# Spatial attention on TensorE: eight heads by four contiguous keys in a block, mixing on 64x32 tiles

## The reference, cut to what matters

```
q, k, v = split(layernorm(h) @ w_qkv.T + b_qkv)          # 8 heads, width 8
dots  = q . k                                            # 94 x 94 for each head
grass = (qr(q).Q . qr(k).Q) ** 2 * grassman_scale
a = concat([dots * scale, dots ** 2 * riem_scale, grass])  # 24 maps
a = batchnorm(a)                                         # constants per map
a = conv_w (8 x 24) @ a + conv_b                         # mixes the 24 maps into 8
out = softmax(a, over keys) @ v ; out @ w_proj.T + b_proj
```

## Time and profile before

| | |
|---|---|
| median of 3 runs | 1019.79 us (1017.86 to 1020.41) |
| the profiled execution | 1019.19 us, span 1017.5 us |
| TensorE matmul busy / weight load busy | 898.6 us (88%) / 577.8 us (57%) |
| VectorE busy | 763.6 us (75%) |
| GpSimd busy | 488.2 us (48%) |
| ScalarE busy | 423.6 us (42%) |
| mean granted TensorE clock | 0.944 |
| instructions | 37672 |

### The profile page before, as it was taken

One profiled execution on the slowest core, in us unless ns is written; L12 is line 12 of the kernel. 1 busy time (PEld: TensorE's weight loads), 2 busy tenths in 40 slices (PEclk: granted clock), 3 DMA queues, 4 the chain that ended last, 5 costly groups with the idle time before them and its releaser, 6 DMA issues. The chain is left out here.

```text
span 1017.5 us, 37672 instructions
## 1 busy us (share of the span) xinstructions
PE 898.6 (88%) x15018; PEld 577.8 (57%) x15018; DVE 763.6 (75%) x1287; ACT 423.6 (42%) x710; POOL 488.2 (48%) x551
## 2 busy tenths in 40 slices
PE   3677668998937999999999999999999999799995
PEld 2233245555525666666666666666666666446663
DVE  4588863887983888888788888888888888747773
ACT  2333423112713444444444444444444444257774
POOL 3355631110007666666666666666666666212220
PEclk9777877998977999999999999999999999979998
DMA  8765000324102111111111111111111111001111
GB/s 300 263 223 202 1 0 1 55 54 115 31 0 64 50 49 50 52 52 52 48 45 48 50 52 52 52 49 46 48 49 50 52 52 53 2 3 29 29 29 32
DMA packets 64446, 63.25 MB, mean 62 GB/s; under 512 B 37081, under 2 KB 55068, under 8 KB 64412
## 3 DMA queue, kind: packets, MB, share of 16 engines
q1 hardware_dynamic: 63884, 61.25, 20.4%
q10 hardware_dynamic: 528, 1.54, 0.4%
HBM read 52.93 MB, written 6.75 MB: 59 GB/s over the span
## 5 line engine op out<-in xcount | busy, mean ns | idle before, releaser
L1163 ACT ACTIVATE sq<-ps_dot 128x752 f32<-128x752 f32 x192 | 153.1, 798 | 302.6 <-PE ps_dot L1042 302.6
L1042 PE MATMUL ps_dot<-q_st,k_blk 32*64 32x94 f32 x6144 | 169.4, 247 | 3.1 <-POOL k_blk L1002 3.1
L1042 PEld LDWEIGHTS ps_dot<-q_st,k_blk 32*64 32x64 f32 x6144 | 134.4, 133 | 64.6 <-issue 50.0
L1002 POOL TENSOR_TENSOR k_blk<-k_turn,hmask 128x384 f32<-128x384 f32 x64 | 65.3, 1020 | 177.8 <-ACT k_turn L1151 177.8
L1210 DVE TENSOR_REDUCE sums<-prob 128x94 f32<-128x564 f32 x128 | 148.0, 1201 | 2.0 <-ACT prob L1156 2.0
L1006 POOL TENSOR_TENSOR k_mix<-k_cm,cols 128x768 f32<-128x768 f32 x64 | 119.8, 1872 | 0.0
L988 POOL TENSOR_TENSOR v_blk<-v_rep,vmask 128x384 f32<-128x384 f32 x128 | 106.6, 854 | 6.8 <-PE ps_m L1074 6.8
L1091 PEld LDWEIGHTS ps_a<-q_st,k_mix 64*64 64x64 f32 x3072 | 77.1, 132 | 56.4 <-issue 48.2
L1091 PE MATMUL ps_a<-q_st,k_mix 64*64 64x94 f32 x3072 | 101.0, 250 | 0.8 <-DVE prob L1198 0.8
L1156 ACT ACTIVATE prob<-prob,cols 128x564 f32<-128x564 f32 x128 | 91.1, 758 | 20.4 <-DVE prob L1198 20.4
L1181 DVE TENSOR_REDUCE row_max<-ps_a 128x94 f32<-128x564 f32 x128 | 89.3, 741 | 12.4 <-PE ps_a L1110 12.4
(11 more groups left out here) (225 smaller groups left out, 1389.7 us busy)
## 6 DMA issues: line engine op xcount, KB each, us to landing
v_rep<-v_rows SPq DMA_DIRECT2D x256, 96.0 KB
x_g<-in_x_dram SPq DMA_DIRECT2D x15, 1500.0 KB, 6.7
v_rows<-tok SPq DMA_DIRECT2D x32, 96.0 KB
q_st<-q_cm SPq DMA_DIRECT2D x64, 47.0 KB
out_dram<-rows SPq DMA_DIRECT2D x16, 188.0 KB
x_g<-in_x_dram ACTq DMA_DIRECT2D x1, 1500.0 KB, 7.4
top_rows<-tok SPq DMA_DIRECT2D x16, 32.0 KB
top<-top_rows SPq DMA_DIRECT2D x1, 512.0 KB, 3.4
```

The source lines that it names most:

```text
L1002: return pool.tensor_tensor(k_blk[:, a, :, kind], view.unsqueeze(2).broadcast_to([128, NTAU, 4, 8]), k["hmask4"][:].unsqueeze(1).unsqueeze ...
L1042: mm = pe.matmul(ps_dot[64 * hg:64 * hg + 64, (a + g) % 2, b, col:col + N], k_blk[rows, a, 2 * (2 * g + t2) + mi].rearrange("p k h m -> p ...
L1163: act.activation(sq[:, :, :, 2 * g:2 * g + 2, :].rearrange("p mi b t n -> p b mi (t n)"), ps_dot[:, (a + g) % 2, :, 0:4 * N].rearrange("p ...
```

## The change

Keys are taken in contiguous order: key = 6 x + t with x from 0 to 15, for which k is stored in another order by the projection (`queries_keys`). A dot block now holds eight heads by four keys (`k_blk`: 24 blocks of 2 kinds x 8 heads x 4 keys), so that a dot matmul uses all 64 rows of a recording (64x64 tiles) and its result has the squared plain dots and the orthogonal ones as partitions (kind, head, 4 keys). Mixing turns 64 such partitions into 32 (4 keys x 8 heads): 16 matmuls a pair of 282 columns on 64x32 tiles. The logits' partitions become (x, head), in four banks of `ps_a`; `ps_dot` has three banks. The constants `mix_w`, `head_const`, `pad_bias`, `den_w` and `vmask` follow this order. The turned keys are made two pairs ahead into `ps_m`, and VectorE builds their blocks straight from PSUM, as its last work of a step; ScalarE's copy is gone. The sums over the six tiles are gone: GpSimd adds tiles 0 to 2 and 3 to 5 (`halves`), and the denominators are three accumulating matmuls per recording. Exponentials are split in two instructions, the last two tiles with a bias that removes the padding. The loops of TensorE and SyncE are written out for all 64 pairs. v is stored and loaded with half as many transfers.

```diff
+            def key_blocks(i, a):                               # VectorE
+                dve.wait_ge(s["kt_done"], i + 1)
+                if later(i, 2):
+                    dve.wait_ge(s["dots_done"], 3 * (i - 1))
+                dve.tensor_tensor(k_blk[:, a, :, 1], ps_m[:, KT_AT:KT_AT + NP]..., k["hmask"]..., ALU.mult)
...
+            def halves(j, a):                                   # GpSimd
+                pool.wait_ge(s["exp_done"], 2 * j + 2)
+                if later(j, 1):
+                    pool.wait_ge(s["av_done"], j)
+                pool.tensor_tensor(half[:], prob[:, a, :, 0:3, :], prob[:, a, :, 3:6, :], ALU.add).then_inc(s["half_done"], 1)
+
+            def build(i, a, n, has_next2):
+                if later(i, 3):
+                    halves(i - 3, 1 - a)
+                if later(i, 2):
+                    pool.wait_ge(s["keyed"], 2 * (i - 1))
+                pool.tensor_tensor(k_blk[:, a, :, 0], k_cm..., k["hmask"]..., ALU.mult).then_inc(s["keys_ready"], 1)
+                pool.tensor_tensor(k_mix[:, a]..., k_cm..., k["conv1"]..., ALU.mult).then_inc(s["mix_ready"], 1)
+                if has_next2:
+                    turning(i + 2, a)
                 if later(i, 1):
                     values(i - 1, 1 - a, n)
...
+                for c in range(SLOTS):                          # TensorE, dots
+                    for v in range(2):
                         for b in range(2):
+                            rows = slice(64 * b, 64 * b + 64)
+                            mm = pe.matmul(ps_dot[64 * v:64 * v + 64, (2 * g + b) % 3, N * c:N * c + N],
+                                           k_blk[rows, a, SLOTS * (3 * v + g) + c]..., q_st[rows, a, :], start=True, stop=True)
...
+            def denominators(j):
+                pe.wait_ge(s["half_done"], j + 1)
+                for t in range(3):
+                    for b in range(2):
+                        mm = pe.matmul(ps_m[64 * b:64 * b + 64, DEN_AT:DEN_AT + N], k["den_w"][:], half[:, b, t, :], ...)
...
+            def squares_mixed(i, b, v):
+                for c in range(SLOTS):
+                    mm = pe.matmul(ps_a[32 * c:32 * c + 32, 2 * b + v, 0:3 * N], k["mix_w"][64 * v:64 * v + 64, :],
+                                   sq[64 * v:64 * v + 64, b, c]..., start=False, stop=True, skip_group_check=True)
                 return mm
+            def mixing(i):
+                pe.wait_ge(s["squared"], 6 * i + 5)
+                squares_mixed(i, 0, 0)
+                pe.wait_ge(s["keyed"], 2 * i + 1)
+                squares_mixed(i, 0, 1).then_inc(s["mixed"], 1)
+                pe.wait_ge(s["squared"], 6 * i + 6)
+                squares_mixed(i, 1, 1)
+                pe.wait_ge(s["keyed"], 2 * i + 2)
+                squares_mixed(i, 1, 0).then_inc(s["mixed"], 1)
+            def step(i, a):
                 dots(i, a, 0)
+                if i + 2 < PAIRS:
+                    turn_keys(i + 2, a)
+                if i >= 1:
                     turn_max(i - 1)
                 dots(i, a, 1)
+                if i >= 1:
                     spread_max(i - 1)
+                if i >= 2:
+                    attended(i - 2, a)
+                    denominators(i - 2)
                 dots(i, a, 2)
+                linear(i, a)
+                mixing(i)
...
+            def step(i, a, has_prev, has_prev2, has_next2):     # ScalarE
                 if has_prev:
+                    act.wait_ge(s["mixed"], 2 * i)
+                squares(i, 0)
+                squares(i, 1)
+                if has_prev:
+                    exps(i - 1, 1 - a, 0)
+                squares(i, 2)
+                if has_prev:
+                    exps(i - 1, 1 - a, 1)
...
-            def sums_of(prev, a):
-                for b in range(2):
-                    dve.wait_ge(s["exp_done"], 2 * prev + b + 1)
-                    dve.tensor_reduce(sums[:, b, :], prob[:, a, b].rearrange("p t n -> p n t"), AX.X, ALU.add).then_inc(s["sum_done"], 1)
+            def step(i, a, has_prev, has_prev2, has_next2):     # VectorE
                 if has_prev:
                     maxima(i - 1)
+                if has_prev:
+                    heads_max(i - 1)
                     shifted(i - 1, 1 - a)
+                if has_prev2:
+                    output(i - 2)
+                if has_next2:
+                    key_blocks(i + 2, a)
```

More of the change, by code:

```diff
@@ L970, in load @@
                 for b in range(2):
-                    src = v_dram[span(2 * i + b, 1)].rearrange("b mi (mj t) f -> mi mj (b t f)", t=NT)
-                    for mi in range(2):
-                        sp.dma_start(v_rep[64 * mi:64 * mi + 64, a, b, :], src[mi].unsqueeze(0).broadcast_to([8, 8, NT * C])).then_inc(v_in[a], 16)
-            load(0, 0)
-            load(1, 1)
-            with sp.Fori(1, PAIRS // 2) as twice:
-                load(2 * twice, 0)
-                load(2 * twice + 1, 1)
+                    src = v_dram[span(2 * i + b, 1)].rearrange("b (x t) f -> x (b t f)", t=NT)
+                    sp.dma_start(v_rep[:, a, b, :], src.unsqueeze(1).broadcast_to([16, H, NT * C])).then_inc(v_in[a], 16)
+            for i in range(PAIRS):
+                load(i, i % 2)
         @block.gpsimd
@@ L1010, in build @@
                 if later(i, 1):
                     values(i - 1, 1 - a, n)
-            build(0, 0, 0)
-            build(1, 1, 1)
-            with pool.Fori(1, PAIRS // 2) as twice:
-                build(2 * twice, 0, twice)
-                build(2 * twice + 1, 1, twice + 1)
+            turning(0, 0)
+            turning(1, 1)
+            for i in range(4):
+                build(i, i % 2, (i + 1) // 2, True)
+            with pool.Fori(2, PAIRS // 2 - 1) as twice:
+                build(2 * twice, 0, twice, True)
+                build(2 * twice + 1, 1, twice + 1, True)
@@ L1119, in step @@
-            def step(i, a, has_prev, has_prev2, has_next):
+                for t in range(NT):
+                    for b in range(2):
+                        for w in range(2):
+                            half_of = slice(64 * w, 64 * w + 64)
+                            mm = pe.matmul(ps_a[half_of, 2 * b + t // 3, N * (t % 3):N * (t % 3) + N],
+                                           k_mix[64 * b:64 * b + 64, a, t, 8 * w:8 * w + 8].rearrange("p x o -> p (x o)"), q_st[64 * b:64 * b + 64, a, :],
+                                           start=(t % 3 == 0), stop=False, skip_group_check=True)
+                        if t == NT - 1:
+                            mm.then_inc(s["keyed"], 1)
@@ L1129, in step @@
-                if has_prev2:
-                    attended(i - 2, a, False)
-                    denominators(i - 2, i)
-                else:
-                    logits_free(i)
-                mixing(i, a)
-            turn_keys(0, 0)
-            steps(pe, step)
+                linear(i, a)
+                mixing(i)
+            for i in range(2):
+                turn_keys(i, i)
+            for i in range(PAIRS):
+                step(i, i % 2)
             turn_max(PAIRS - 1)
             spread_max(PAIRS - 1)
-            attended(PAIRS - 2, 0, False)
@@ L1141, in _ @@
[L1141 to L1143 removed]
+            for j in (PAIRS - 2, PAIRS - 1):
+                attended(j, j % 2)
+                denominators(j)
         @block.scalar
         def _(act):
[L1147 to L1151 removed]
```

261 lines of the change are left out of this document (108 added, 153 removed).

## The result

The change makes the kernel slower: 1052.76 us median of four runs (1048.35 to 1053.39) against 1019.75, a ratio of 1.0319, 95% interval 1.0293 to 1.0345. The prediction was 941, with 0.88 on faster. The profiled execution took 1052.94 us, its span is 1051.3 us, its mean granted clock 0.909 where before had 0.944.

A forecast was written before the change was run, and what follows sets the result against it. The bound was a closed loop of TensorE and VectorE taking turns, 8.87 us a pair. TensorE's new terms summed to 7.60; 61 x 1.27 = 77.5 plus 1.5 at the ends, 79 off 1019.8, gave 941 us, range 918 to 992.

The forecast's parts named there:

- from the reduction to the spread there are 0.87: TensorE's loop, transposes term: 0.87 us from VectorE's reduction over the heads to the spread, part of 1.33.
- a GpSimd busy some 95% of the period: GpSimd in the attention stage: 7.25 us of work in a 7.60 us period, with a short wait each pair.
- 7.60: TensorE's forecast period in us per pair, spread to spread, in the attention stage, where it had been 8.87.
- mixing: TensorE's 16 mixing matmuls per pair: eight tiles at once, two sets of 0.55, 1.10 us instead of 2.51.
- (B): Rival on TensorE's mixing: four tiles at once at most, mixing 2.20, period 8.70, 1008 us; chance 0.13.
- (D): Slower rival: column tiles over one row half go two by two, mixing 4.4, period 10.9, 1142 us; chance 0.07.
- 16 x 0.55 = 8.8: TensorE's mixing by the skill's row-group rule, column tiles following one another: some 8.8 us; the prediction did not adopt it.
- (A): Rival: GpSimd becomes the bound at 7.3 to 8.1 us a pair, never idle; 971 us at 8.1; chance 0.14.
- the written-out loops: Unrolled loops of TensorE and SyncE, straight code for all pairs: forecast to change nothing.
- (E): Rival of no change: mixing near 2.37, or a new 1.27 us wait in the loop; chance 0.03.
- (C): Rival: VectorE's 7.07 us period is reached because TensorE's tile-shape changes cost less; 908 us; chance 0.05.
- if VectorE idles for something not listed here: Closing sign that the prediction is wrong: unlisted idle time on VectorE; no size given.

The follow-up runs named there:

- the wait on GpSimd: Changed kernel, copies kept, plus one wait: GpSimd starts a pair's key blocks only after VectorE's copies of the pair before; 921.96 us, ratio 0.9048.
- The run without the orthogonal maps: Changed kernel with GpSimd waiting for the copies, and only 8 of 16 mixing matmuls, on one row half; 933.12 us in a single run.
- the contiguous copies: Changed kernel with its two VectorE copies kept as copies but written in contiguous order instead of with a stride; 1061.02 us, ratio 1.0402.
- The kernel before with the extra product: Kernel before the change with one more GpSimd product of 384 elements a pair, result unused, behind `k_mix`; 1063.27 us, ratio 1.0423.

## Why the prediction was wrong

**The step that failed** is in the sum: "from the reduction to the spread there are 0.87". That term came from the one period shown in the earlier trace rows, where the copies run 0.15 us behind GpSimd's `k_mix`. In the changed kernel it is 611.02 to 613.53 = 2.51, with the copies at 2.00 where they had 0.36. The same text forecast a GpSimd busy some 95% of the period, without asking which VectorE instructions would then lie beside its work. The sign was in the trace of before: one line with a minimum of 211 ns and a maximum of 1265.

With that term the sum comes out. 7.60, plus 1.64 for the term, less 0.28 for the others of TensorE (the transposes among them), is 8.96, the undisturbed period. The clock, which I had carried at 1.00, adds 0.48, for 9.44. The change without the collision is the 921.96 of the wait on GpSimd, against 941 forecast, at the lower edge of the forecast's own 922 to 957.

**TensorE's terms**, as (forecast, after): mixing 1.10, 1.21; linear 1.22, 1.08; third dots 0.81, 0.70; attended 1.03, 1.02; denominators 0.60, 0.59; turned keys 0.39, 0.30. Eight tiles at once, which no row of before showed, held. The run without the orthogonal maps shows it, and so (B) and (D) are out as causes. The Trainium skill, "TensorE: Matmul & The Clock Gate", section "The mechanism", ties the overlap of a weight load to another row group, and has matmuls start strictly in written order; four tiles over the same rows go side by side here, with 1.08 us for eight matmuls of 282 columns, and the row halves that were written one behind the other took 1.27, under the 1.6 of strict order. The prediction's 16 x 0.55 = 8.8 put all sixteen one behind the other; with the row halves side by side, as the rule on the row group leaves them, it would be an estimated 8 x 0.55 = 4.4. Neither came.

**VectorE's terms**: key block 0.98, 0.96; subtractions 1.50, 1.40. **GpSimd's**: `k_blk` 1.96, 1.51; `k_mix` 1.89, 1.51; halves 1.33, 1.18; values 1.67, 1.66; in all 7.25 forecast, some 6.3 measured, 65% of the stage and not 95. Both products were sized by the old pattern's rows and run faster in the new one. (A), GpSimd as the bound, did not come: it idles 0.89 us ahead of the halves and 1.99 ahead of the values. It did its harm without being the bound.

**ScalarE** at 5.0 (six squares of 0.48, two exponentials of 0.61 and two of 0.44) and **the written-out loops** at nothing were right, the latter shown by a run of its own.

**The rivals**: none of the five was it. (E) had the kind, a new wait in the loop, at 0.03, but with denominators behind late halves as its only example, and with 1.27 us for no change where 1.64 came. (C) is not what the best version shows either: VectorE's loop has 7.02 there for the 7.07 forecast, but it waits 0.34 ahead of the maxima, and TensorE, busy 443.8 of 450 us, sets the 7.36. All five asked what each engine does by itself. The one that was missing asks what two engines do to each other. The text came closest in its own way to fail, "if VectorE idles for something not listed here", without a price, and even that sign would not have shown: VectorE counts as busy through its slow copies, and the idle time is TensorE's.

What stays open: why the clock falls in some pairs and not in others with the same wait of 1.68 us, and more often with the contiguous copies (0.92 over the stage for 0.94).

## What to carry to other kernels

Price an instruction from rows whose neighbours are doing what they will be doing afterwards. A tiny instruction whose maximum is many times its minimum is the sign, and what ran beside its slow cases names the cause. When an edit fills an engine that shares something with another, list the other's short instructions on the critical loop that will fall into the newly busy time. And an idle wait put on the engine that has slack may be the cheapest repair there is: one line made this kernel 12.4% faster than the change alone (921.96 against 1052.76), and 9.5% faster than before.

## What the runs showed of the hardware

- A VectorE copy of 128 elements between SBUF tiles takes 0.21 to 0.22 us (0.27 in the changed kernel's pattern) with GpSimd idle, and up to 1.60 us beside GpSimd's elementwise products; two of them stood to the end of a product of 1.51 us and through the whole of the next. A reduction of length one over the same data takes 0.38 us beside the same products, and 256 elements take 0.61 us, in one instruction or in two that overlap.
- Idle time on TensorE cost twice here. A gap of 1.68 us a pair took the granted clock from 1.00 to 0.94 over the stage, and six unused matmuls in it gave back 34 us. The kernel before with the extra product has a gap of 0.77 us a pair and kept 1.00.
- Eight 64x32 tiles work at once, and the order in which the row halves are written matters little to the matmuls themselves: mixing took 1.21 us in alternating order and 1.27 with the halves one behind the other. It matters to what waits for them, at 0.62 us a pair.
- GpSimd's product of 768 elements takes 1.51 us in the new order of keys and 1.89 in the old, so its cost depends on more than the count.
